# Two-layer conditioned residual on one core: the prologue rebuilt so that x leads SyncE's queue and one table holds w1 and the bias

## The reference

```python
def _L0_cond_ref(x, conditions, weights):      # 200 matrices
    w = weights[conditions]
    return jnp.einsum('bct,bcd->bdt', x, w)
def _L1_cond_ref(x, subjects, weights, bias):  # 8 matrices, 8 bias rows
    w = weights[subjects]
    b = bias[subjects]
    out = jnp.einsum('bct,bcd->bdt', x, w)
    out = out + b[:, :, None]
    return out
x = x + _L0_cond_ref(x, itok_B_1_198, L0_cond_weights)
x = x + _L1_cond_ref(x, itok_B_0_7, L1_cond_weights, fside_8xS_0)
```

## Time and profile before

| | |
|---|---|
| median of three runs | 355.75 us |
| the profiled execution's own time | 356.31 us |
| its span, first to last instruction | 354.5 us |
| TensorE busy (matmul) | 279.4 us, 79% |
| VectorE busy | 126.7 us, 36% |
| ScalarE busy | 96.9 us, 27% |
| GpSimd busy | 68.9 us, 19% |
| moved by DMA | 140.87 MB, mean 397 GB/s |

### The profile page before, as it was taken

One profiled execution on the slowest core, in us unless ns is written; L12 is line 12 of the kernel. 1 busy time (PEld: TensorE's weight loads), 2 busy tenths in 40 slices (PEclk: granted clock), 3 DMA queues, 4 the chain that ended last, 5 costly groups with the idle time before them and its releaser, 6 DMA issues.

```text
span 354.5 us, 5415 instructions
## 1 busy us (share of the span) xinstructions
PE 279.4 (79%) x770; PEld 133.9 (38%) x770; DVE 126.7 (36%) x207; ACT 96.9 (27%) x135; POOL 68.9 (19%) x264
## 2 busy tenths in 40 slices
PE   0069999967968966977985985998788796997784
PEld 0034545423424523533533533453344343443341
DVE  1214544513424431441441441444134252442432
ACT  0023335312322320530331321443034132231322
POOL 1054221122112111311212213221121221221200
PEclk9999999989989998996998996999699899898999
DMA  4999999999999999999999999999999999999966
GB/s 166 363 392 395 348 407 414 415 415 414 418 415 418 415 418 415 408 416 415 409 417 419 411 418 421 415 419 415 419 414 417 420 418 418 416 415 418 416 269 245
DMA packets 50014, 140.87 MB, mean 397 GB/s; under 512 B 3924, under 2 KB 16726, under 8 KB 50006
## 3 DMA queue, kind: packets, MB, share of 16 engines
q1 hardware_dynamic: 31108, 73.61, 53.2%
q10 hardware_dynamic: 18898, 67.18, 46.7%
HBM read 76.09 MB, written 67.11 MB: 404 GB/s over the span
## 4 chain that ended last, share of the span: by engine, by line
SPq 54%; DMA 22%; issue 11%; PE 10%; DVE 1%; ACT 1%; ACTq 1%; POOLq 0%; POOL 0%; DVEq 0%
SPq L115 27%; DMA xy<-x 13%; SPq L133 12%; PE y_ps L242 8%; SPq L110 6%; DMA out<-xy 5%; SPq L130 5%; SPq L116 4%; DMA w_sb<-w 4%; PE m_ps L225 1%; ACT xy L334 1%; DVE j_all L295 0%; POOLq L185 0%; SPq L153 0%; ACTq L348 0%
## 5 line engine op out<-in xcount | busy, mean ns | idle before, releaser
L242 PE MATMUL y_ps<-xy,m_sb 128*128 128x512 f32 x512 | 256.7, 638 | 51.1 <-DMA xy<-x 50.2
L242 PEld LDWEIGHTS y_ps<-xy,m_sb 128*128 128x128 f32 x512 | 95.4, 202 | 159.6 <-issue 130.4
L310 DVE TENSOR_SCALAR xy<-y_ps,j_pick 128x512 f32<-128x512 f32 x128 | 96.1, 751 | 154.1 <-PE y_ps L242 154.1
L334 ACT ACTIVATE xy<-y_ps,j_pick 128x512 f32<-128x512 f32 x128 | 87.9, 687 | 227.0 <-PE y_ps L242 226.6
L192 POOL COPY w_pick<-w_home 128x128 f32 x128 | 37.5, 293 | 266.1 <-issue 266.1
L225 PEld LDWEIGHTS m_ps<-j_pick,w_pick 128*128 128x128 f32 x256 | 43.7, 214 | 47.6 <-issue 34.2
L225 PE MATMUL m_ps<-j_pick,w_pick 128*128 128x128 f32 x256 | 43.4, 297 | 11.5 <-POOL j_pick L194 11.5
L302 DVE TENSOR_TENSOR m_sb<-m_ps,j_pick 128x256 f32<-128x256 f32 x64 | 27.2, 425 | 55.0 <-PE m_ps L225 55.0
L194 POOL COPY j_pick<-j_all 128x129 f32 x128 | 37.8, 295 | 0.0
L334 ACT ACT_TABLE_LOAD x7 | 9.0, 1283 | 26.7 <-POOL j_pick L194 20.2
L248 PE MATMUL home_ps<-eye,home_less_b 128*1 128x128 f32 x2 | 0.6, 397 | 8.1 <-DVE home_less_b L279 8.1
(11 more groups left out here) (6 smaller groups left out, 0.7 us busy)
## 6 DMA issues: line engine op xcount, KB each, us to landing
xy<-x SPq DMA_DIRECT2D x63, 1024.0 KB, 19.9
out<-xy ACTq DMA_DIRECT2D x63, 1024.0 KB, 9.2
w_home<-w_t SPq DMA_DIRECT2D x128, 64.0 KB
xy<-x SPq DMA_DIRECT2D x4, 256.0 KB, 19.5
w_sb<-w ACTq DMA_DIRECT2D x1, 512.0 KB, 13.1
out<-xy SPq DMA_DIRECT2D x2, 256.0 KB, 3.9
out<-xy ACTq DMA_DIRECT2D x2, 256.0 KB, 3.6
cond_rows<-cond ACTq DMA_DIRECT2D x1, 64.0 KB, 4.1
```

What stands on the lines that cost most here:

```text
L242: nc.tensor.matmul(y_ps[:, b % YB, h, :], m_sb[:, s, k, :], xy[:, s, k, half(h)], start=True, stop=True).then_inc(y_ready, 1)
L310: nc.vector.tensor_scalar(xy[:, s, k, half(0)], y_ps[:, b % YB, 0, :], j_pick[:, s, k, D:D + 1], None, ALU.add).then_inc(left_out[b % YB], 1)
L334: nc.scalar.activation(xy[:, s, k, half(1)], y_ps[:, b % YB, 1, :], ACT.Identity, bias=j_pick[:, s, k, D:D + 1]).then_inc(right_out[b % YB ...
```

## The change

SP issues slot 0 of `x` as its first DMA. `first_words` now goes over ACT's queue, as the first one there, and has two rows: the first 16 indices of the first layer and the first 16 of the second. SP then waits for it and issues, for each slot, the two matrices of this slot and after them the next slot of `x`. `load_words` goes to the end of ACT's prologue DMAs.

The second layer's matrices and the bias come as one array `w1_bias`, laid out on the host by channel, then matrix, 129 values each. It is loaded straight into `j_all`, as ACT's second DMA; `w1_sb` and `bias_sb` are gone. DVE adds the unit matrix in place with one instruction over all 8, ahead of the work on the homes. POOL has a `pick_first` for round 0: it reads the second layer's index from `first_words` and takes W0 from the fixed place of its own batch entry, and waits for the homes only after round 0.

```diff
-    w1_sb = sb("w1_sb", [C, N1, D])
-    bias_sb = sb("bias_sb", [D, N1])
-    first_words = sb("first_words", [1, ROUND_B], I32)
+    first_words = sb("first_words", [1, 2, ROUND_B], I32)
...
-            sp.dma_start(first_words[:], cond0[:, 0:ROUND_B]).then_inc(first_loaded, 16)
-            sp.dma_start(load_words[:].rearrange("o b f -> o (b f)"), cond0_twice).then_inc(cond0_loaded, 16)
-            for s in range(LEAD):
-                load_x(0, s)
+            load_x(0, 0)
             sp.wait_ge(first_loaded, 16)
-            for s in range(LEAD):
+            for s in range(RING):
                 load_w0_first(s)
-            for s in range(LEAD, RING):
-                load_w0_first(s)
-                load_x(0, s)
+                if s < LAST:
+                    load_x(0, s + 1)
...
+            def pick_first(s):
+                pool.wait_ge(w0_loaded[s], PAIR * 16)
+                _, words = nc.values_load_multi_w_load_instructions(
+                    first_words[0:1, 1, s * PAIR:(s + 1) * PAIR], engines=(mybir.EngineType.Pool,),
...
+                for k in range(PAIR):
+                    i = nc.s_assert_within(words[k], 0, N1 - 1)
+                    nc.gpsimd.tensor_copy(w0_pick[:, s, k, :], w0_home[:, s * PAIR + k, :])
+                    last = nc.gpsimd.tensor_copy(
+                        j_pick[:, s, k, :], j_all[:, bass.ds(i, 1), :].rearrange("c n d -> c (n d)"))
+                last.then_inc(picked, 1)
...
-            pool.wait_ge(cond1_loaded, 16)
-            pool.wait_ge(home_ready, 2)
-            pool.wait_ge(bias_in_j, 1)
+            pool.wait_ge(first_loaded, 16)
             pool.wait_ge(j_ready, 1)
             for s in range(RING):
-                pick(0, s)
+                pick_first(s)
+
+            pool.wait_ge(home_ready, 2)
...
+            dve.wait_ge(w1_loaded, 16)
+            dve.wait_ge(eye_ready, 1)
+            nc.vector.tensor_tensor(j_all[:, :, 0:D], j_all[:, :, 0:D],
+                                    eye[:].rearrange("c (o d) -> c o d", o=1).to_broadcast([C, N1, D]), ALU.add)\
+              .then_inc(j_ready, 1)
             dve.wait_ge(cond0_compared, 32)
...
-            dve.wait_ge(bias_loaded, 16)
-            nc.vector.tensor_copy(j_all[:, :, D:D + 1], bias_sb[:].rearrange("d (n o) -> d n o", o=1))\
-              .then_inc(bias_in_j, 1)
-            dve.wait_ge(w1_loaded, 16)
-            dve.wait_ge(eye_ready, 1)
-            for n in range(N1):
-                last = nc.vector.tensor_tensor(j_all[:, n, 0:D], w1_sb[:, n, :], eye[:], ALU.add)
-            last.then_inc(j_ready, 1)
...
+            act.dma_start(first_words[:].rearrange("o f b -> o (f b)"), first).then_inc(first_loaded, 16)
+            act.dma_start(j_all[:].rearrange("c n d -> c (n d)"), w1_bias.rearrange("c n d -> c (n d)"))\
+               .then_inc(w1_loaded, 16)
             act.dma_start(cond0_rows[:], cond0.to_broadcast([B, B])).then_inc(cond0_compared, 16)
             act.dma_start(cond0_col_sb[:], cond0_col).then_inc(cond0_compared, 16)
             act.dma_start(pick_words[:].rearrange("o b f -> o (b f)"), cond1_twice).then_inc(cond1_loaded, 16)
-            act.dma_start(bias_sb[:], bias_t).then_inc(bias_loaded, 16)
-            act.dma_start(w1_sb[:], w1.rearrange("n c d -> c n d")).then_inc(w1_loaded, 16)
+            act.dma_start(load_words[:].rearrange("o b f -> o (b f)"), cond0_twice).then_inc(cond0_loaded, 16)
```

More of the change, by code:

```diff
@@ L9, with conditioned_residual_kernel @@
 ACT = mybir.ActivationFunctionType
-def conditioned_residual_kernel(nc, x, cond0, cond0_col, cond0_twice, cond1_twice, bias_t, w0_t, w1, out):
+def conditioned_residual_kernel(nc, x, cond0, cond0_col, first, cond0_twice, cond1_twice, w0_t, w1_bias, out):
     B, C, T = x.shape
     N0, _, D = w0_t.shape
-    N1 = w1.shape[0]
+    N1 = w1_bias.shape[1]
     assert C == D == 128
@@ L84, in conditioned_residual_kernel @@
         w1_loaded = sem("w1_loaded")
-        bias_loaded = sem("bias_loaded")
         x_loaded = [sem(f"x_loaded{s}") for s in range(RING)]
@@ L92, in conditioned_residual_kernel @@
         eye_ready = sem("eye_ready")
-        bias_in_j = sem("bias_in_j")
         j_ready = sem("j_ready")
@@ L119, in load_w0_first @@
             def load_w0_first(s):
-                words = words_of(first_words[0:1, s * PAIR:(s + 1) * PAIR])
+                words = words_of(first_words[0:1, 0, s * PAIR:(s + 1) * PAIR])
                 for k in range(PAIR):
@@ L180, in _ @@
         def _(pool):
+            def pick_first(s):
+                pool.wait_ge(w0_loaded[s], PAIR * 16)
+                _, words = nc.values_load_multi_w_load_instructions(
+                    first_words[0:1, 1, s * PAIR:(s + 1) * PAIR], engines=(mybir.EngineType.Pool,),
+                    skip_runtime_bounds_check_because="each word is checked against its own range below")
+                for k in range(PAIR):
[4 more added lines that the diff above has]
+                last.then_inc(picked, 1)
             def pick(r, s):
@@ L380 @@
         "cond0_col": np.ascontiguousarray(itok_B_1_198).reshape(-1, 1),
+        "first": np.concatenate([np.asarray(itok_B_1_198)[:16], np.asarray(itok_B_0_7)[:16]]).reshape(1, -1),
         "cond0_twice": np.repeat(np.asarray(itok_B_1_198), 2).reshape(1, -1),
         "cond1_twice": np.repeat(np.asarray(itok_B_0_7), 2).reshape(1, -1),
-        "bias_t": np.ascontiguousarray(np.asarray(fside_8xS_0).T),
         "w0_t": np.ascontiguousarray(np.asarray(L0_cond_weights).transpose(0, 2, 1)),
-        "w1": np.ascontiguousarray(L1_cond_weights),
+        "w1_bias": np.concatenate([np.asarray(L1_cond_weights).transpose(1, 0, 2),
+                                   np.asarray(fside_8xS_0).T[:, :, None]], axis=2),
     }
```

## The result

The changed kernel takes 353.46 us (median of nine runs, 352.91 to 354.93), the kernel before 355.75. The ratio is 0.9950, with a 95% interval of 0.9939 to 0.9961: faster by 0.5%. The forecast was 351.1, so the direction was right and the size too large: 4.7 us forecast, 2.3 us measured by the medians and 1.8 by the ratio. The two differ because the nine runs spread (four of them lie at 354.0 or above) and the ratio goes by their mean. The profiled execution took 353.38 us, 2.9 less than that of the kernel before, and its span is 351.6 us against 354.5.

The account below looks back on a forecast made before the run. DMA traffic, with one trailing engine of 16, was taken as the bound. Start 2.7, w1 and bias 0.6 and first store 1.4 us sum to 4.7, giving a median of 351.1 us; range 349.9 to 353.7 with the first two rivals and bounds.

Parts of the forecast that it names:

- The bound: Whole kernel: DMA traffic bounds it, PE has time to spare, and one of 16 engines trails the others in loads.
- The start, 2.7 us: First loads of `x`: slot 0 moves 3.3 us sooner, less 0.3 for tables and 0.3 for a dry spell; bounds 0.7 to 3.3.
- The row for slot 0: Start of the kernel: slot 0's first data at 1.75 us against 5.05, 3.3 us sooner.
- the rival of a late `first_words`: Start: `first_words` lands late while SP waits, holding matrices and slots 1 to 7; slower, 357.6 us; chance 0.06.
- the prediction's own sign of failure: Changed profile: a traffic hole at 5 to 7 us would mean late `first_words`; a hole growing by the start's gain, a wrong prediction.
- The first rival: Start: only the issue time is won, 0.7 us, giving 2.7 us in all and 353.1 us; chance 0.13.
- w1 and the bias, 0.6 us: Traffic at 10 to 15 us: longer rows for w1 and bias win 0.6 us; bounds 0.3 and 0.9.
- The first store, 1.4 us: Traffic at 37 to 46 us: an earlier first store removes the 343 GB/s stretch, 1.4 us; bounds 0 and 1.6.
- Costed at nothing: Homes after the start: later tables have 8 us of cover, and the shorter `pick_first` hides behind PE; 0 us.
- The sum: Whole kernel: 2.7 + 0.6 + 1.4 = 4.7 us off the profiled 356.31, median 351.1 us.

Follow-up runs that it names:

- homes_on_pe: Changed kernel without the two tables of 128 rows; indices come as one row, spread by two small PE products: 352.27 us, ratio 0.9895.
- w1_alone: Kernel before, with only `w1_bias` loaded and added in one piece at w1's old place: 354.22 us, ratio 0.9957.
- store_late: Changed kernel, but POOL waits for the matrices of slot 3 before its first pick: 357.76 us, ratio 1.0047.
- tables_late: Changed kernel, but ACT holds the four small tables back until the matrices of slot 0 have landed: 353.38 us, ratio 0.9931.
- x1_first: Changed kernel, but SP issues slots 0 and 1 of `x` before it waits for `first_words`: 354.06 us, ratio 0.9949.
- order_alone: Kernel before, with only the new order of first DMAs; w1, bias and picks stay old: 355.64 us, ratio 0.9985.
- col_thrice: Changed kernel, but the table of 128 rows of 4 bytes is loaded three times, twice into spare buffers: 355.26 us, ratio 0.9987.

## Why the prediction was wrong in size

*The bound* was read rightly: DMA traffic, and one engine of 16 that trails. The traces show the trailing directly. The semaphore of a load is counted up in 16 steps, which I take for one from each engine. For the loads of slots that land before 46 us, the sixteenth step comes at most 0.3 us after the fifteenth in the kernel before and 0.1 in the changed one. From there the distance grows, to a mean of 4.8 and 3.9 us for loads landing around 200 us and to 10.9 and 11.0 us for the last quarter MB.

*The start, 2.7 us: this is the step that failed.* The row for slot 0 was right: it moved 3.2 us sooner (forecast 3.3), and `first_words` landed at 1.99, so the rival of a late `first_words` is out. But the prediction said that slot 1, issued at 4.8, "can move at about 5.7". I had just found that slot 0 had been held by "the work ahead of it", two tables of 128 rows, and did not ask who stands behind them once slot 0 doesn't. Slot 1 does. Measured, the start brought 0.65 us of traffic by 10 us; the missing 2 us are the hole, and homes_on_pe, in which the tables are gone, has 303 GB/s instead of 220 in the first 10 us, 2.0 us more. So the prediction's own sign of failure came true, a hole that took back what the start had won, though it had put a hole there down to a late `first_words`. The first rival, only 0.7 us won at the start and 353.1 us, has nearly the measured numbers, but by luck: its condition, that slot 0 still takes 3.5 us, did not hold. The rule of the Trainium skill (DMA: Bandwidth & Descriptors, Issuing engines are not separate DMA queues), which would have given this term 0.7 us, was near the measured number. The way there is another one: what held slot 0 was not a full set of DMA engines, which stood still, but the order in which DMAs begin.

*w1 and the bias, 0.6 us:* measured 0.8 us in 10 to 15 us, and in w1_alone, where nothing else of the start differs, 5 x (383 - 337) / 416 = 0.55 us. J was ready at 8.26 (forecast 7.5), the one add took 1.23 us (1.2).

*The first store, 1.4 us:* measured 1.4 us in 37 to 46 us, and store_late shows the cause. The store itself came at 22.13 instead of 19.8. POOL began its picks at 11.38, since the matrices of slot 0 sat in the hole; without the hole, in homes_on_pe, it began at 9.42; the forecast had it begin at 7.5, with J. SP loaded slot 0 again at 31.85, not at 26 to 29. The margin was smaller than I had written, and it held.

*Costed at nothing:* true in the changed kernel, but for a reason that I had not checked. PE's product for the homes stands ahead of its first real product; it ran at 11.12, 1.3 us ahead of it. tables_late shows what it costs when that cover goes.

*The sum.* The prediction took a gain in the mean for a gain at the end, on the ground that the trailing engine "has worked without a pause wherever it had loads to do". The table has the kernels in order of what the mean was ahead at 300 us, with the kernel before at the foot, by (GB/s - 403) x 300 / 416, which the rounding of the rates makes uncertain by up to 0.7 us. Beside it stands how much shorter the span of the same execution was than 354.5, then (1 - ratio) x 355.75, which goes by all executions, and last how long after the fifteenth step the sixteenth came for the last quarter MB of `x`.

| kernel | GB/s to 300 us | 37 to 46 us | ahead in the mean | ahead at the end, same execution | at the end, by the ratio | sixteenth step behind |
|---|---|---|---|---|---|---|
| homes_on_pe | 411 | 417 | 5.8 | 3.7 | 3.7 | 8.2 |
| changed | 408 | 408 | 3.6 | 2.9 | 1.8 | 11.0 |
| x1_first | 408 | 415 | 3.6 | 1.6 | 1.8 | 11.7 |
| w1_alone | 407 | 417 | 2.9 | 1.2 | 1.5 | 12.2 |
| order_alone | 407 | 416 | 2.9 | 0.7 | 0.5 | 13.7 |
| col_thrice | 406 | 408 | 2.2 | 0.2 | 0.5 | 13.2 |
| tables_late | 406 | 372 | 2.2 | 2.8 | 2.5 | 7.9 |
| store_late | 401 | 333 | -1.4 | -1.6 | -1.7 | 9.8 |
| before | 403 | 343 | 0 | 0 | 0 | 10.9 |

Five kernels lose 1.7 to 2.2 us between 300 us and the end of the same execution. In four of them the trailing engine is further behind at the end than in the kernel before; homes_on_pe is the exception. The changed kernel's profiled execution loses 0.7, no more than the rounding, and tables_late, where the engine is 3.0 us less behind than before, loses nothing. My reading, which homes_on_pe doesn't fit in full, is that what the mean wins reaches the end less what the trailing engine has lost meanwhile. How much that is differs from kernel to kernel; why this engine trails, and which of the 16 it is, stays open. That it catches up in the dip, which would explain why the kernels with a dip lose nothing, doesn't come out of the traces: in the kernel before it is at most 0.3 us behind when the dip begins, so there is nothing to catch up.

In the profiled executions the forecast 4.7 us come apart like this: 2.05 us less at the start, 0.2 more for w1, some 0.75 more in the stretches between, which no term had and which is within the rounding, and 0.7 less at the end, which gives the 2.9 measured (356.31 - 353.38). The hole is thus nearly the whole miss there. Over all executions the gain is smaller, 1.8 by the ratio: the changed kernel's runs spread over 2.0 us, those of the kernel before over 0.8. The slower ones have no trace, so where they lost it is not shown.

## What to carry to other kernels

When a transfer starts late though the DMA engines are idle, look at what was issued ahead of it on any queue, above all tables of one short row per partition. Moving the transfer ahead of them only hands the wait to the next one, and moving the tables takes the wait along. Bring such a table in as one row and spread it with a small product: that gave the fastest kernel here. And before a gain in mean traffic is booked at the end, look whether one DMA engine of the 16 trails (a share near one sixteenth with loads still awaited, as the 0.07 of the earlier trace rows): then a part of the gain can be lost again before the end, here up to 2.2 us.

## What the runs showed of the hardware

- In the starts traced here, DMAs of SP and ACT moved in the order of issue, over both queues. Each further table of 128 rows of 4 bytes, 512 bytes in all, made the hole some 0.7 us longer (col_thrice). One such table and one of 128 rows of 512 bytes together left a hole of 2 us, wherever they were issued (6.5 to 8.5 us in the changed kernel, 12.5 to 14.5 in tables_late), although 1 MB loads had been issued ahead of them. Matrices of 128 rows of 512 bytes left none (404 GB/s in 6 to 9 us of homes_on_pe).
- The first `x` rows moved slowly: share 0.87 at 66 GB/s in 1.5 to 2.0 us, and 401 GB/s from 3.0 on.
- The last of the 16 steps by which a load is counted in came at most 0.3 us after the fifteenth for the loads of slots that landed before 46 us, in the kernel before and the changed one, and 10.9 and 11.0 us after it for the last quarter MB of `x`; over the nine kernels of the table this last figure goes from 7.9 to 13.7 us.
- 32 rows of 4096 bytes on each of 7 engines cost 5.2 us, on each of 15 engines 5.4 us, if the rows lie on the engines as I expect.
